# Expert tiles in three feed-forward layers: a fixed first tile per expert, loads without a wait, and a two-part search in the last layer

## What is computed

```python
# layer 0: nearest of 8 centroids, one expert of 8 per token, gated SiLU (hidden 512)
# layer 1: softmax scores, top 2 of 8 experts, clipped swiglu, plus a shared expert
# layer 3: top 2 of 6 experts, gelu (hidden 512):
gate_logits = jnp.einsum('bsd,de->bse', x, Wg) + bg
topk_w, topk_idx = jax.lax.top_k(gate_logits, TOP_K)
topk_w = jax.nn.softmax(topk_w, axis=-1)
combine = jnp.sum(jax.nn.one_hot(topk_idx, NUM_EXPERTS) * topk_w[..., None], axis=-2)
h = jax.nn.gelu(jnp.einsum('bsd,edh->ebsh', x, W1) + b1[:, None, None, :], approximate=False)
y = jnp.einsum('ebsh,ehd->ebsd', h, W2) + b2[:, None, None, :]
out = jnp.einsum('ebsd,bse->bsd', y, combine)
```

## Time and profile before

| | us |
|---|---|
| median of 3 runs | 1898.63 (1898.32 to 1901.4) |
| profiled execution | 1896.64 |
| its span, first to last instruction | 1894.8 |
| TensorE busy in the span | 1775.1 (94%) |
| VectorE busy | 1047.9 (55%) |
| ScalarE busy | 843.6 (45%) |
| GpSimd busy | 555.6 (29%) |
| mean granted TensorE clock | 0.981 |

### The profile page before, as it was taken

How to read it: one execution, slowest core, us unless ns; L and a number is a source line. 1 busy time by engine, 2 the same in 40 slices (tenths; PEclk the granted TensorE clock), 3 DMA queues, 4 the chain that set the end, 5 groups by cost and what they waited for, 6 DMA issues and landing times.

```text
span 1894.8 us, 42986 instructions
## 1 busy us (share of the span) xinstructions
PE 1775.1 (94%) x16790; PEld 1384.3 (73%) x16790; DVE 1047.9 (55%) x2665; ACT 843.6 (45%) x2411; POOL 555.6 (29%) x596
## 2 busy tenths in 40 slices
PE   8999889999989989899999989999799899998998
PEld 6886669944767846699999967777544577766787
DVE  7787751263376348775555545556765655447411
ACT  6664542232276343333333335555511566635332
POOL 5441133200155213301222113332202456515242
PEclk9999889999999999999999999999899999999999
DMA  4221069671025010141999642111011455300397
GB/s 152 52 63 34 23 207 319 235 222 52 22 52 140 21 57 3 55 176 64 333 337 328 229 148 75 52 47 61 4 56 61 117 156 152 100 1 2 132 350 248
DMA packets 88303, 234.02 MB, mean 124 GB/s; under 512 B 10176, under 2 KB 45664, under 8 KB 81600
## 3 DMA queue, kind: packets, MB, share of 16 engines
q1 hardware_dynamic: 78416, 210.61, 33.3%
q0 software_dynamic: 5664, 15.47, 2.5%
q10 hardware_dynamic: 4048, 5.52, 0.9%
HBM read 216.35 MB, written 12.07 MB: 121 GB/s over the span
## 4 chain that ended last, share of the span: by engine, by line
PE 73%; DVE 11%; ACT 5%; DMA 5%; issue 4%; POOL 1%; SPq 0%; ACTq 0%; POOLq 0%; PEldq 0%; DVEq 0%; PEld 0%
PE PS L1137 15%; PE PS L1606 6%; PE PS L1148 5%; PE PS L3678 3%; PE PS L3182 3%; PE PS L3703 3%; PE PS L3498 3%; PE PS L3190 3%; PE PS L2402 2%; ACT l1x_probs L2532 2%; PE PS L2757 2%; PE PS L3215 2%; DMA l1x_probsT<-in_ctx_dram 2%; DMA weights<-in_experts_up_dram 1%; PE PS L2473 1%
## 5 line engine op out<-in xcount | busy, mean ns | idle before, releaser
L2361 POOL TENSOR_TENSOR l1x_probs<-l1x_probs,l1x_total 128x512 f32<-128x512 f32 x64 | 68.5, 1092 | 192.4 <-DVE l1x_total L2607 192.4
L1606 PE MATMUL PS<-weights,l0x_ctxT 128*128 128x256 f32 x512 | 120.5, 386 | 0.0
L1137 PE MATMUL PS<-l1f_xT,l1f_slot 128*128 128x128 f32 x1024 | 117.0, 275 | 0.0
L1137 PEld LDWEIGHTS PS<-l1f_xT,l1f_slot 128*128 128x128 f32 x1024 | 115.7, 192 | 0.1
L1606 PEld LDWEIGHTS PS<-weights,l0x_ctxT 128*128 128x128 f32 x512 | 94.2, 190 | 14.6 <-issue 2.1
L3152 POOL TENSOR_TENSOR l2x_probs<-l2x_probs,l2x_total 128x512 f32<-128x512 f32 x64 | 65.0, 1038 | 129.6 <-DVE l2x_total L3348 129.6
L95 PE MATMUL PS<-consts 128*128 128x256 f32 x320 | 79.3, 392 | 1.2
L2532 ACT ACTIVATE l1x_probs<-PS,l1x_top 128x257 f32<-128x257 f32 x128 | 59.0, 474 | 39.3 <-DVE l1x_top L2602 39.3
L1264 DVE SCALAR_TENSOR_TENSOR l1f_product<-PS,l1f_slot,l1f_side 128x128 f32<-128x128 f32 x128 | 36.0, 344 | 65.9 <-ACT l1f_side L1220 65.9
L1090 POOL DMA_INDIRECT l1f_out_dram<-l1f_out,l1f_sort_target_row x23 | 22.7, 986 | 159.5 <-DVE l1f_out L1247 159.5
L3678 PE MATMUL PS<-l3x_keysT,l3x_QW 128*128 128x289 f32 x256 | 67.7, 407 | 1.7 <-issue 1.7
(11 more groups left out here) (661 smaller groups left out, 4588.6 us busy)
## 6 DMA issues: line engine op xcount, KB each, us to landing
l1f_slot<-in_experts_up_dram SPq DMA_DIRECT2D x16, 2056.0 KB, 10.0
weights<-in_experts_up_dram SPq DMA_DIRECT2D x8, 2056.0 KB, 10.2
l0f_slot<-in_experts_up_dram SPq DMA_DIRECT2D x15, 1024.0 KB, 7.7
weights<-in_experts_down_dram SPq DMA_DIRECT2D x21, 640.0 KB, 5.9
l1f_slot<-in_experts_down_dram SPq DMA_DIRECT2D x16, 640.0 KB, 4.8
l0x_ctxT<-in_ctxT_dram SPq DMA_DIRECT2D x32, 257.0 KB, 2.6
l2x_ctxT<-in_ctxT_dram SPq DMA_DIRECT2D x32, 257.0 KB, 2.7
l3x_ctxT<-in_ctxT_dram SPq DMA_DIRECT2D x32, 257.0 KB, 2.7
```

The costliest lines, as they stand in the source:

```text
L1137: done = nc.tensor.matmul(PS[:, bank + a, m * P:(m + 1) * P], mat[:, c, m * P:(m + 1) * P], x, start=(c == 0), stop=(c == 1))
L1606: last = nc.tensor.matmul(PS[:, 2 * (b % 2) + k, half * D:(half + 1) * D], ctxT[b % SLOTS][:, c, half * P:(half + 1) * P], kw[:, c, k * D: ...
L2361: nc.gpsimd.tensor_tensor(p, p, bcast(total[b % 2][:, 2 * n:2 * n + 2], 2, KEYS), ALU.mult).then_inc(probs_done, 1)
```

## The change

- **Fixed first tiles.** In all three layers tile e (e < E) is now the first tile of expert e, and the T - E other tiles follow, in the order of experts. `place_rows` gets the arithmetic for that (three more instructions on VectorE, and one that no longer overlaps with the next), `weight_row` lists only the T - E others.
- **Loads.** SP waits for `done` only at tile E and reads no expert's number before it. In layers 0 and 1 the loads of tiles 0 to 2 follow the store of the rows at once.
- **Layer 3, two tiles preloaded.** `load_first_tiles` loads up and down weights of tiles 0 and 1 at the start of the self-attention stage before; TensorE waits for `first_tiles_in` once.
- **Layer 0.** `place_weights` moves behind `mark_columns`.
- **Layer 3, ranks.** A scan on VectorE sums `chosen` over the tiles, TensorE adds the rest (`near_tensor`), so the large product and sum over tiles (L842, L843) go. The rows of the first E tiles are found by a search of their own (`place_near`, `find_near`), and `tokens_found` is raised for them; then come the marks of the others, `place_weights`, the second search (`find_far`) and `place_far`, which writes the other token rows and all targets. The one-hot columns are written four groups at a time, columns of the first four ahead of the near marks. `keep_busy` goes from 6, 18, 8 to 6, 4, 3, with none behind the second search. ScalarE's code isn't changed.

```diff
@@ load_first_tiles, called in layer 3's self attention behind load_next(sp)
+    for i in range(tiles):
+        sp.dma_start(mem[:, i * whole:i * whole + up_width], core.dram[f"experts{layer}_up"][i]).then_inc(core.first_tiles_in, 16)
+        sp.dma_start(mem[:, i * whole + up_width:(i + 1) * whole], core.dram[f"experts{layer}_down"][i]).then_inc(core.first_tiles_in, 16)
@@ Places
+    def near_tensor(self, pe, chosen, chosen_done):
+        pe.wait_ge(chosen_done, 1)
+        pe.wait_ge(self.named, 2)
+        nc.tensor.matmul(by_tile, self.later[:], chosen, start=True, stop=False)
+        pe.wait_ge(self.summed_up, 1)
+        nc.tensor.matmul(by_tile, self.ones[:], self.so_far[:].rearrange("p e t -> p t e"), start=False, stop=True)
+        nc.tensor.matmul(PS[:, 4, n:n + E], self.ones[:], self.so_far[:, :, NT - 1], start=True, stop=True).then_inc(self.counted, 1)
+    def find_near(self, pe, columns):
+        pe.wait_ge(self.near_marked, 1)
+        for n in range(N):
+            if n % 4 == 0:
+                pe.wait_ge(self.column_done, n // 4 + 1)
+            done = nc.tensor.matmul(PS[:, 5, 0:self.K * self.E], columns[:, n, 0:P], self.marked_near[:, n].rearrange("p m i -> p (m i)"), start=(n == 0), stop=(n == N - 1))
+    def find_far(self, pe, columns):
+        pe.wait_ge(self.far_marked, 1)
+        for n in range(N):
+            done = nc.tensor.matmul(PS[:, 3, 0:self.K * (self.T - self.E)], columns[:, n, 0:P], self.marked_far[:, n].rearrange("p m i -> p (m i)"), start=(n == 0), stop=(n == N - 1))
@@ Places.place_rows (layers 0 and 1)
-        nc.vector.tensor_tensor(self.places[:], self.before[:], by_tile(PS[:, 4, 0:n]), ALU.add)
-        step(nc.vector.tensor_scalar(self.count[:], self.start[:], float(P), None, ALU.mult))
-        step(nc.vector.tensor_tensor(self.places[:], self.places[:], bcast(self.count[:], 1, NT), ALU.add))
+        step(nc.vector.tensor_tensor(self.places[:], self.before[:], by_tile(PS[:, 4, 0:n]), ALU.add))
+        self.further_tiles(dve, self.count[:])
+        step(nc.vector.scalar_tensor_tensor(self.count[:], self.start[:], float(P), by_expert, ALU.mult, ALU.subtract))
+        step(nc.vector.tensor_scalar(self.count[:], self.count[:], float(P * (E - 1)), None, ALU.add))
+        step(nc.vector.scalar_tensor_tensor(self.before[:], self.places[:], float(P), bcast(self.count[:], 1, NT), ALU.is_ge, ALU.mult))
+        step(nc.vector.tensor_tensor(self.places[:], self.places[:], bcast(by_expert, 1, NT), ALU.add))
+        step(nc.vector.tensor_tensor(self.places[:], self.places[:], self.before[:], ALU.add))
@@ SortedExperts.load
-        sp.wait_ge(places.done, 1)
-        for i in range(T):
+        for i in range(self.preloaded, T):
             j = (S + i) % RING
-            row = self.core.nc.values_load(places.weight_row[0:1, i:i + 1], ...)
+            row = i * P
+            if i == self.E:
+                sp.wait_ge(places.done, 1)
+            if i >= self.E:
+                row = self.core.nc.values_load(places.weight_row[0:1, i - self.E:i - self.E + 1], ...)
@@ l3_feed_forward, TensorE
-            ex.places.tensor(pe, chosen, chosen_done)
-            core.keep_busy(0, 18)
-            ex.places.find_tensor(pe, ex.gathered)
-            core.keep_busy(7, 8)
+            ex.places.near_tensor(pe, chosen[:].rearrange("p e t -> p t e"), chosen_done)
+            core.keep_busy(0, 4)
+            ex.places.find_near(pe, ex.gathered)
+            core.keep_busy(7, 3)
+            ex.places.find_far(pe, ex.gathered)
+            pe.wait_ge(core.first_tiles_in, 32 * FIRST_TILES)
             ex.tensor(pe, core.HT)
```

More of the change, by code:

```diff
@@ new lines, in place_far @@
+    def place_far(self, dve):
+        nc, PS, E, T = self.core.nc, self.core.PS, self.E, self.T
+        step = lambda instruction: self.core.dve_step(dve, instruction)
+        dve.wait_ge(self.tokens_found, 1)
+        dve.wait_ge(self.far_found, 1)
+        step(nc.vector.tensor_scalar(self.found_row[:, E:T], PS[:, 3, T - E:2 * (T - E)], -1.0, 0.0, ALU.add, ALU.max))
+        nc.vector.tensor_copy(self.token_row[:, E:T], self.found_row[:, E:T]).then_inc(self.tokens_found, 1)
+        dve.wait_ge(self.tokens_found, 2)
+        nobody = self.nobody[:].rearrange("p a r -> p (a r)")[:, 0:T]
+        for tiles, targets in ((slice(0, E), PS[:, 5, 0:E]), (slice(E, T), PS[:, 3, 0:T - E])):
+            step(nc.vector.scalar_tensor_tensor(self.found_row[:, tiles], targets, 0.0, nobody[:, tiles], ALU.is_equal, ALU.mult))
+            step(nc.vector.scalar_tensor_tensor(self.found_row[:, tiles], targets, -1.0, self.found_row[:, tiles], ALU.add, ALU.add))
+        nc.vector.tensor_copy(self.target_row[:], self.found_row[:]).then_inc(self.targets_found, 1)
+        dve.wait_ge(self.targets_found, 1)
@@ L858, in place_rows, with further_tiles @@
             step(nc.vector.reduce_sum(self.place[:, k, :], self.before[:], AX.X))
+    def further_tiles(self, dve, count):
+        nc, E = self.core.nc, self.E
+        step = lambda instruction: self.core.dve_step(dve, instruction)
+        over, earlier = self.pairs[:, 0, :, 1:NT], self.pairs[:, 1, :, 0:E]
+        step(nc.vector.tensor_tensor(over, bcast(count, 2, NT - 1), bcast(self.core.numbers[:, 1:NT], 1, E), ALU.is_gt))
+        step(nc.vector.reduce_sum(self.tiles[:], over, AX.X))
+        step(nc.vector.tensor_tensor(earlier, bcast(self.tiles[:], 1, E), self.core.before[:, 0:E, 0:E], ALU.mult))
+        step(nc.vector.reduce_sum(self.start[:], earlier, AX.X))
     def place_weights(self, dve):
-        nc, E, T = self.core.nc, self.E, self.T
+        nc, E, T = self.core.nc, self.E, self.T - self.E
         step = lambda instruction: self.core.dve_step(dve, instruction)
@@ L1036, in nth, with loads, wait_weights @@
         return q + (1 - (self.S - j + RING - 1) // RING)
+    def loads(self, q, j):
+        return self.nth(q, j) - (j < self.preloaded)
+    def wait_weights(self, pe, q, j, loaded):
+        if not isinstance(q, int) or RING * q + j >= self.preloaded:
+            pe.wait_ge(loaded[j], 16 * self.loads(q, j))
     def sorted_next(self, n, shared):
@@ L1052, in load @@
         down_read = self.down_done if self.kind == "glu" else self.out_copied
-        sp.wait_ge(places.done, 1)
-        for i in range(T):
+        for i in range(self.preloaded, T):
             j = (S + i) % RING
-            row = self.core.nc.values_load(places.weight_row[0:1, i:i + 1], engines=[mybir.EngineType.SP],
-                                           skip_runtime_bounds_check_because="the number of the expert is clamped to the last one on VectorE")
+            row = i * P
+            if i == self.E:
+                sp.wait_ge(places.done, 1)
+            if i >= self.E:
+                row = self.core.nc.values_load(places.weight_row[0:1, i - self.E:i - self.E + 1], engines=[mybir.EngineType.SP],
+                                               skip_runtime_bounds_check_because="the number of the expert is clamped to the last one on VectorE")
             if i >= RING:
```

126 lines of the change are left out of this document (100 added, 26 removed).

## The result

The changed kernel takes **1908.77 us** (median of 5 runs, 1905.57 to 1914.11) against 1898.63 before: a ratio of 1.0062, 95% interval 1.0045 to 1.0078. The two medians lie 10.1 us apart; by the ratio it is 11.8 us, or 0.6%. I had forecast 1900.5 and no change, with a range up to 1905.0. The profiled execution took 1908.77 us with a span of 1907.0, so the span grew by 12.2 us.

The account below looks back on a forecast made before the run. Ahead of the first sorted tile, neither TensorE's peak nor weights bound it, but chains of waits. Layer 0 -0.5, layer 1 +0.8, layer 3 +1.6 made +1.9: 1898.5 profiled, 1900.5 us median; range 1895.5 to 1905.0.

Parts of the forecast that it names:

- Layer 0, the context batches: Layer 0: six batches share engines with early loads, land by 277 us; TensorE works until 282.5, hidden by the gather.
- both bounds: Layer 0, time per context batch: about 1.4 us alone, up to 3.6 us beside the loads.
- context batches starve: Slower rival, layer 0: last batch at 282 us, not 277; +2.2 instead of -0.5 us, 1903.2 in all; chance 0.12.
- my sum: Layer 0 in all: -0.5 us, from -5.9 to +2.2.
- Layer 0, the gathers and the list: Layer 0: gather 1 lands 0 to 4 us earlier, taken as 0.5; list behind columns, token row unchanged within 0.1 us.
- Layer 1: Layer 1: more rank steps on VectorE ahead of shared tile 1's products, nothing covers them: +0.8 us (0.7 to 0.9).
- Layer 3, the order of waits: Layer 3: ScalarE waits for `weighed`, makes sixteen diagonals, only then copies tile 0; rows found early wait in SBUF.
- Layer 3, sizes: Layer 3: `weighed` at 1786.8 us (+0.7), cold first tiles +1.3, 0.4 absorbed: +1.6 us, from -0.6 to +5.5.
- the clock falls in the first search: Slower rival, layer 3: first search at half clock from its start, diagonals +4.4, with cold start +5.5; 1904.4 us; chance 0.16.
- What I held unchanged: Stages the change doesn't touch were to stay as they were; one of them moving was a sign of being wrong.
- the two slower rivals: Layer 3's clock falling in the first search (0.16) and layer 0's context batches starving (0.12): 1904.4 and 1903.2 us.
- my signs of being wrong: Layer 3 diagonals over 2 us earlier, layer 0 gathers landing in 3 us, or a stage held unchanged moving.

Follow-up runs that it names:

- e5: Kernel before the change, with ScalarE's sixteen diagonals of layer 3 moved behind the last tile; ratio 1.0005 to the kernel before.
- e1: Changed kernel, with layer 0's first six load transfers held until the first one-hot column is written; ratio 1.0015 to the kernel before.
- e10: e6 with one undivided search in layer 3, and layer 1's tiles numbered as before the change; ratio 0.9980 to the kernel before.
- e4: Changed kernel, with layer 0's first three tiles of weights let go one at a time; ratio 1.0023 to the kernel before.
- e3: Changed kernel, with ScalarE's sixteen diagonals of layer 3 moved behind the last tile; ratio 1.0018 to the kernel before.
- e6: Changed kernel with the edits of e4 and e3 together; ratio 0.9982 to the kernel before.
- e8: Changed kernel, with VectorE's three `odds` steps in layer 3 ahead of its wait for the first search; ratio 1.0021 to the kernel before.
- e11: Changed kernel measured again without an edit; ratio 1.0053 to the kernel before.

## Why the prediction was wrong

**Layer 0, the context batches: the step that failed.** I let four batches be outstanding at 268 us and gave them 2.2 us each, so 277. In the trace the first of the six landed at 269.8, so all six were outstanding, and the last at 283.1: 2.65 us each over the five that followed. The rows had both bounds (1.4 and 3.6 us), and the rival "context batches starve" had the mechanism and nearly the landing (282). Its price was too small as well: I took 5.46 us for the 24 products behind the wait, and they took 8.18. That row of before was itself a good one, since in e5, the old order, they took 7.14, and 7.15 in e1. The effect was +6.0 us counted from the gate, +4.7 at the stage's end in this trace, where the rival had +2.2 and my sum -0.5. The Trainium skill ("DMA: Bandwidth & Descriptors", "Queues, rings and completion order") says that each transfer engine takes turns between the queues that have work for it. The trace agrees in so far as the batches were slowed and not shut out, but beside the loads that meant 11.1 us instead of 3.0 to 3.8. I had taken that sentence for a reason to stay near the lower bound; it gives no size.

**Layer 0, the gathers and the list.** They landed 6.1 and 5.7 us after issue (before 6.8 and 7.4), no longer the last thing waited for. The list behind the columns left the token row where it was, to 0.1 us, as said.

**Layer 1: right.** +0.83 us in the trace, and e10 took it away again.

**Layer 3, the order of waits: right.** The diagonals decided, ScalarE's wait was ended by `odds`, and the rows found ahead waited for them. The scan took 0.26 us (I had 0.3).

**Layer 3, sizes: the other step that failed.** `weighed` was to come 16.8 us behind the end of `chosen`, and came 20.5 behind. Of these 3.7 us, 2.0 are the second search (6.87 for 4.83, and more than the 6.2 that I had for half clock), up to 0.9 the first (4.38 for 3.5), and 0.65 the counting products, stuck behind fillers at half clock; e5 shows that the old order can lose these 0.65 too. The first two tiles cost 2.3 us for their cold products (3.62 + 2.60 against twice 1.95) where I had 1.3. The rival "the clock falls in the first search" said diagonals 4.4 us later, and 4.4 it was, but partly by luck. It had the first search at half clock from its start, 6.2 us; in the traces the first search of layer 3, or the only one, fell on its way and took 3.77 to 5.11 us, in all kernels. In place of that came a slower second search and the late counts. I gave it 0.16, and the part that mattered was the rule: the second search took 6.87 in all seven traces that kept its place and its fillers (changed, e1, e3, e4, e6, e8, e11). My evidence against it, 3.50 us in layer 1, came from a stage where dense products run around the search.

**What I held unchanged.** Pieces of half clock in stages that the change doesn't touch moved the traces both ways, by about 1 us in the changed kernel's and by over 3 in e4's. They don't explain the median: the changed kernel, measured twice, gave 1.0062 and 1.0053, and with both faults repaired 0.9982. They do limit what one trace can carry: the 7.0 us from router to counts and the 5.46 us of layer 0, on which I built, were the best of all traces.

**The chances.** I gave the two slower rivals 0.28 together and left both at once outside the range, as a tail. Both effects came, each with its own sizes, and by my prices both together make 1900.5 + 2.7 + 3.9 = 1907.1 us, past my upper bound of 1905.0 and 1.7 below the measured time. That this is so near is luck: layer 0's price was too small, layer 3's (5.5 against 5.0 from the counts to the end) slightly too large. Nor did my signs of being wrong look this way: they named earlier diagonals and faster gathers, not diagonals that start over 2 us later.

## What to carry to other kernels

Before a load is let go early, list what is then in flight on every other queue and who waits for it. A load that isn't needed yet belongs behind the transfers that are, and one load at a time can be both early and harmless. When a result is made available sooner, follow it to its first reader: if a wait for something later stands in between in the reader's order, nothing is gained, and moving three steps or one block may give all of it. A search split in two saves only if its second half fits a gap, for on the engine that is the bound it is simply more work.

## What the runs showed of the hardware

- A transfer of 257 KB took 3.8 us (median of seven, e1) ahead of a backlog and 11.1 us (median of six) beside six loads of 4.7 MB in all on another queue. In the second case the engines moved 380 to 401 GB/s in total, more than the 253 of the earlier trace rows, so they weren't slower, only shared.
- The 24 products of 257 columns took 8.18 us after 9.29 us of idling, 7.02 after 10.98, and 5.46, 7.14 and 7.15 with no idle time worth the name (before, e5, e1). So their clock could fall without an idle time as well, and the length of the idle time didn't set the price.
- The same products ahead of layer 3's counts (router and twelve filler instructions) ran at full clock in one trace of the old order (3.63 and 2.84 us) and fell on the way in the other (4.57 and 5.24; granted clock 0.79 and then 0.52).
- A first-to-last scan over 48 elements a partition took 0.26 us, where other steps of 48 took 0.20 to 0.24.
